# A four-layer graph network on one core: part of the first layer's row work handed to GpSimd, counts and degrees in one PSUM bank, chain steps issued in halves

## The reference

```python
x = LN(x + L0(x))   # relu([x, (adj@x + x)/deg] @ W + b), rows divided by their L2 norm; deg = rowsum(adj) + 1
x = LN(x + L1(x))   # tanh([x, t]@W1 + b1)@W2 + b2 + adj@(x@B.T) - rowsum(adj)*(x@B.T)
x = LN(x + L2(x))   # w@(x@weight) + bias; w[i,j] = adj[i,j] * 0.5**(min(deg, 100) - pos)
                    # pos: the rank of neighbour j among i's, less what is over 100
x = LN(x + L3(x))   # logmap(adj @ expmap(x)) @ kernel + bias
```

## Time and profile before

| | |
|---|---|
| median of 3 runs | 173.23 us (172.87 to 173.72) |
| profiled execution | 172.62 us, of which the span of the trace is 170.8 us |
| PE busy | 110.9 us (65%), 1230 matmuls |
| DVE busy | 105.7 us (62%), 235 instructions |
| ACT busy | 70.8 us (41%) |
| POOL busy | 46.3 us (27%) |
| HBM read | 18.00 MB |

### The profile page before, as it was taken

How to read it: one execution, slowest core, us unless ns; L and a number is a source line. 1 busy time by engine, 2 the same in 40 slices (tenths; PEclk the granted TensorE clock), 3 DMA queues, 4 the chain that set the end, 5 groups by cost and what they waited for, 6 DMA issues and landing times.

```text
span 170.8 us, 3082 instructions
## 1 busy us (share of the span) xinstructions
PE 110.9 (65%) x1230; PEld 63.5 (37%) x1244; DVE 105.7 (62%) x235; ACT 70.8 (41%) x119; POOL 46.3 (27%) x54
## 2 busy tenths in 40 slices
PE   0000279961996498669725979999989989994000
PEld 0000159730243124326402345667446734463000
DVE  0181999889999998950499101535602698718870
ACT  0030215577277556462781285254023310157550
POOL 0000002412421263020148000433500554603380
PEclk9999999997599789999985899999999999999755
DMA  4999999999999910000000000000000000000005
GB/s 97 255 250 345 307 347 263 319 331 333 332 331 339 341 40 4 0 0 4 0 4 0 0 0 4 0 4 2 0 4 0 0 2 0 0 4 0 0 0 123
DMA packets 13950, 18.73 MB, mean 110 GB/s; under 512 B 5360, under 2 KB 5488, under 8 KB 13936
## 3 DMA queue, kind: packets, MB, share of 16 engines
q1 hardware_dynamic: 7728, 9.74, 20.1%
q10 hardware_dynamic: 6208, 8.78, 17.5%
HBM read 18.00 MB, written 0.52 MB: 108 GB/s over the span
## 4 chain that ended last, share of the span: by engine, by line
PE 44%; DVE 26%; ACT 9%; DMA 7%; issue 4%; POOL 4%; SPq 2%; POOLq 1%; another core or an unknown queue 0%; DVEq 0%
PE psN L823 7%; PE psC L823 7%; DMA stage<-adj 7%; PE psS L823 6%; PE psS L880 5%; DVE AT L572 5%; DVE AT L573 4%; ACT WT L402 3%; PE psX L940 2%; POOL nroot L308 2%; PE psX L872 2%; PE psX L852 2%; PE psC L861 2%; PE psH L970 2%; PE psH L971 2%
## 5 line engine op out<-in xcount | busy, mean ns | idle before, releaser
L402 ACT ACTIVATE WT<-psC 128x1024 int16<-128x1024 f32 x32 | 31.3, 1021 | 17.2 <-PE psC L919 17.2
L289 POOL TENSOR_TENSOR root<-var,power 128x4 f32<-128x4 f32 (+1 forms) x16 | 18.9, 1183 | 46.8 <-DVE var L622 22.6
L823 PE MATMUL psS<-AT,XP 128*128 128x512 bf16 x74 | 20.4, 398 | 1.2 <-issue 1.1
L572 DVE STREAM_TRANSPOSE AT<-stage 128x1024 bf16<-128x1024 bf16 x10 | 13.1, 1311 | 11.7 <-DMA stage<-adj 11.7
L872 PE MATMUL psH<-AT,cb 128*32 128x256 bf16 x32 | 1.7, 344 | 19.3 <-DVE AT L573 19.3
L573 DVE STREAM_TRANSPOSE AT<-stage 128x1024 bf16<-128x1024 bf16 x10 | 12.7, 1275 | 0.0
L823 PE MATMUL psN<-AT,XP 128*128 128x512 bf16 x44 | 12.0, 402 | 1.0 <-DVE XP L578 0.7
L638 DVE TENSOR_TENSOR t<-psH,XB 128x256 f32<-128x256 f32 x4 | 1.7, 424 | 17.5 <-PE psH L971 10.2
L823 PEld LDWEIGHTS psS<-AT,XP 128*128 128x128 f16 x80 | 7.3, 101 | 12.4 <-issue 5.9
L302 POOL TENSOR_TENSOR XB<-X,weights 128x256 f32<-128x256 f32 x12 | 9.9, 835 | 7.0 <-DVE X L627 7.0
L914 PE MATMUL psC<-later,cb 32*32 32x512 bf16 x256 | 7.2, 398 | 6.0 <-ACT WT L402 6.0
(11 more groups left out here) (151 smaller groups left out, 229.5 us busy)
## 6 DMA issues: line engine op xcount, KB each, us to landing
stage<-adj SPq DMA_DIRECT2D x20, 256.0 KB, 15.2
stage<-adj ACTq DMA_DIRECT2D x20, 256.0 KB, 11.5
WT<-adj ACTq DMA_DIRECT2D x12, 256.0 KB, 12.7
WT<-adj SPq DMA_DIRECT2D x12, 256.0 KB, 16.9
out<-X SPq DMA_DIRECT2D x6, 64.0 KB, 1.9
weights<-weights_packed SPq DMA_DIRECT2D x1, 353.5 KB, 15.7
cb<-constants_packed SPq DMA_DIRECT2D x1, 264.2 KB, 9.8
X<-x SPq DMA_DIRECT2D x2, 128.0 KB, 7.1
```

Source lines behind the costliest of these rows:

```text
L289: nc.gpsimd.tensor_tensor(root[:, e, 0:n], var[:, e, 0:n], power[:, 0:n, 0:NR], ALU.pow).then_inc(root_ready, 1)
L402: nc.scalar.activation(WT[:, e, tiles], psC[:, PAIRS * h:PAIRS * (h + 1)], ACT.Relu).then_inc(chain_taken, 1)
L572: nc.vector.transpose(to[:, :, :, :, 0], halves[:, :, 0, :, :, 1])
L823: ins = nc.tensor.matmul(sum_bank(l, e), XP[:, l % 2, c], matrix, start=(c == 0), stop=last)
```

## The change

Four things are changed together.

1. **Finishing of chunks 0 and 1.** The squares, the centring, `combine` and the scaling of rows move from DVE to POOL (`square_relu`, `centre_relu`, `combine`, `scale_rows`); relu, the row sums and the split stay on DVE (`relu0`, `sums0`, `variance0`, `split1`), put between the transposes. Chunks 2 and 3 keep the old functions. POOL also centres x for all nodes (`XB`, 128x1024), and `weigh(e + 1)` now stands behind `scale_rows(e)` in POOL's order.
2. **One bank.** Counts, spread and degrees of all chunks use `psH`; `dense(0, e)` uses it too and waits for `deg_taken`.
3. **Chain in halves.** A step is two halves of two quarters (8+8 matmuls each), and a half waits only for its own two banks; the steps stand at other places in TensorE's and ScalarE's order.
4. **Order.** Tile 1 is loaded ahead of the constants; the second half of chunk 0's counts and sums comes before the own parts; only `b1` is centred early, the other six weights between `combine0(3)` and `normalise(0, 3)`.

```diff
 # sync
+            load_lower(1)
             sp.dma_start(cb[:].bitcast(U16), cpack).then_inc(consts_loaded, 16)
             sp.dma_start(weights[:, 0:first], wpack[:, 0:first]).then_inc(own_weights_loaded, 16)
-            for m in range(1, NR - 1):
+            for m in range(2, NR):
                 load_lower(m)
             sp.dma_start(weights[:, first:WTOT], wpack[:, first:WTOT]).then_inc(weights_loaded, 16)
 # gpsimd
+            def square_relu(e):
+                pool.wait_ge(y_ready, e + 1)
+                ye = v[:, chunk(e), 0:D]
+                nc.gpsimd.tensor_tensor(X[:, chunk(e)], ye, ye, ALU.mult).then_inc(ysq_ready, 1)
+            def centre_relu(e):
+                pool.wait_ge(ymean_ready, e + 1)
+                ye = v[:, chunk(e), 0:D]
+                step(nc.gpsimd.tensor_tensor(ye, ye, per_node(ymean[:, chunk(e)]), ALU.add))
+            def combine(e):
+                te = t[:, chunk(e)]
+                pool.wait_ge(ssroot_ready, e + 1)
+                step(nc.gpsimd.tensor_tensor(te, v[:, chunk(e), 0:D], per_node(ssroot[:, chunk(e)]), ALU.mult))
+                step(nc.gpsimd.tensor_tensor(te, te, XB[:, chunk(e)], ALU.add))
+                nc.gpsimd.tensor_tensor(X[:, chunk(e)], te, te, ALU.mult).then_inc(tsq_ready, 1)
+            def scale_rows(e):
+                pool.wait_ge(root_ready, e + 1)
+                nc.gpsimd.tensor_tensor(X[:, chunk(e)], t[:, chunk(e)], per_node(root[:, e, 0]), ALU.mult
+                                        ).then_inc(x_ready, 1)
...
+            pool.wait_ge(xmean_ready, 1)
+            nc.gpsimd.tensor_tensor(XB[:], X[:], per_node(xmean[:]), ALU.add).then_inc(xc_ready, 1)
...
 # vector
+            def relu0(e):
+                dve.wait_ge(dense_taken, e + 1)
+                nc.vector.tensor_scalar(v[:, chunk(e), 0:D], t[:, chunk(e)], 0.0, None, ALU.max).then_inc(y_ready, 1)
+            def sums0(e):
+                cs = chunk(e)
+                dve.wait_ge(y_ready, e + 1)
+                step(nc.vector.tensor_reduce(ymean[:, cs], v[:, cs, 0:D], AX_X, ALU.add))
+                nc.vector.tensor_scalar(ymean[:, cs], ymean[:, cs], -1.0 / D, None, ALU.mult).then_inc(ymean_ready, 1)
+                dve.wait_ge(ysq_ready, e + 1)
+                step(nc.vector.tensor_reduce(ss[:, cs], X[:, cs], AX_X, ALU.add))
+                nc.vector.tensor_tensor(ss[:, cs], ss[:, cs], floor[:, cs], ALU.max).then_inc(ss_ready, 1)
+            def variance0(e):
+                dve.wait_ge(tsq_ready, e + 1)
+                step(nc.vector.tensor_reduce(var[:, e, 1], X[:, chunk(e)], AX_X, ALU.add))
...
+            def split1(e):
+                dve.wait_ge(x_ready, e + 1)
+                split(1, e, X[:, chunk(e)], PART_SCALE[1])
...
 # tensor
             def counts(e, cols=slice(0, CW)):
-                if e == NE - 1:
-                    pe.wait_ge(hid_taken, 2)
-                bank = psH if e == 0 else psX
+                if e >= 1:
+                    pe.wait_ge(dense_taken, e)
...
             def chain(i):
...
-                else:
-                    pe.wait_ge(chain_taken, PAIRS * i)
...
+                for h in range(PAIRS):
+                    if i >= 1:
+                        pe.wait_ge(chain_taken, PAIRS * (i - 1) + h + 1)
+                    for q in range(PAIRS * h, PAIRS * (h + 1)):
...
             def dense(l, e):
                 if l == 0:
+                    pe.wait_ge(deg_taken, e + 1)
...
             pe.wait_ge(transposed, NB)
             counts(e, rest)
             sum_cols(e, 3, 4)
+            transpose_x(1, 1)
+            spread(e)
+            sums(1, 0, range(1, 2))
+            degrees(e)
             chain(10)
-            spread(e)
-            degrees(e)
             dense(0, e)
-            sums(1, 1, range(0, 1))
+            hidden(1)
             chain(11)
-            sums(1, 1, range(1, 2))
+            sums(1, 1, range(0, 2))
             chain(12)
             transpose_x(1, 2)
             sums(1, 0, range(2, 3))
+            chain(13)
             hidden(2)
             sums(1, 1, range(2, 3))
-            chain(13)
+            chain(14)
             sums(1, 0, late)
...
             dense(1, 0)
-            chain(14)
+            chain(15)
             sums(1, 2, every)
             add_own(1, 2)
             dense(1, 1)
-            chain(15)
```

191 lines of the change are left out of this document (99 added, 92 removed).

## The result

The kernel after takes 165.3 us (median of 4 runs, 164.39 to 165.9) against 173.06 (4 runs, 172.87 to 173.72): a ratio of 0.9541, 95% interval 0.9489 to 0.9592. The forecast was 163.9, range 160.3 to 168.5. The profiled execution took 165.22 us, its span is 163.3. Some executions of a kernel take 1.5 to 4% longer than its fastest, mostly at a lower granted clock: ratios and intervals leave them out, the times in the table of the experiments are medians of all, and the profiled executions of dense_late, whole_steps, degrees_first and late_tail are of that kind.

What follows compares the result with a forecast made beforehand. DVE was taken to bound the kernel up to tile 15's last transpose, then a chain of waits between engines. -2.2 - 6.5 - 0.6 = -9.3 us gave 163.3 profiled, 163.9 as median; range 160.3 to 168.5.

Steps and rivals of the forecast that it cites:

- E: End of tile 15's second transpose on DVE: 2.2 us earlier, at about 70.9 (bounds -6 and +3).
- TensorE can hold DVE up at `take_degrees`: DVE may wait for degrees of chunks 1 and 2: 1.2 us added, between 0 and 5.
- Rival 1: TensorE's clock falls in both groups and DVE waits 3 to 5 us for degrees: 166 to 168 us; chance 0.20.
- The other terms of E: DVE's changes up to tile 15's last transpose, without the added wait for degrees: -3.4 us together.
- Contention at the two splits: `split1` of chunks 0 and 1 meets POOL at the memory port: 1.0 us added per chunk (0 to 1.5).
- the six instructions: Row work leaving DVE per early chunk (squares, centring, three of `combine0`, row scaling): 2.7 us, 5.4 for two chunks.
- Before tile 5 nothing is gained: Start of DVE's transposes: reading is saturated, so the end of tile 5's second transpose stays at 33.49 us.
- Rival 4: POOL's port use also holds up DVE's transposes, 13 us in all: 177 us; chance 0.05 with the like.
- E to D: From tile 15's last transpose to the end of layer 1's first `dense`: 6.5 us shorter (bounds -3 and -7.5).
- Rival 3: Behind tile 15, ScalarE's six steps delay its copies and the late sums; only 3 us gained: 167.5 us; chance 0.10.
- Chain: Behind layer 1's first `dense`: one step instead of two, -0.8, plus 0.2 for halves: -0.6 us.
- The other signs: Wait near 2 us for last degrees, chunk 3's split some 18.5 us after tile 15, late sums unwaited, first `dense` 24 us after.

Runs made afterwards that it cites:

- dense_late: The kernel after, with `dense(0, 0)` moved behind the own parts and the first chain step on TensorE; 162.56 us, ratio to before 0.9400.
- whole_steps: The kernel after, with chain steps issued whole again instead of in halves; 164.80 us, ratio to before 0.9492.
- degrees_first: dense_late, with the chain steps of chunks 1 and 2 behind the degrees instead of ahead of them; 163.91 us, ratio to before 0.9436.
- late_tail: dense_late, with six weights centred during DVE's wait for the last degrees and POOL's chunk 2 root ahead of chunk 3's; 161.36 us, ratio to before 0.9292.
- counts_behind_hidden: The kernel after, with the last counts put back behind chunk 1's hidden layer and its tanh; 172.55 us, ratio to before 0.9827.
- pool_finish_2: The kernel before with only POOL's and DVE's new work and order, plus `dense(0, e)` ahead of layer 1's sums; 174.23 us, ratio to before 1.0010.

## Why the prediction was right, and where it was not

**E: -2.2 predicted, 0.0 measured. The term that failed is "TensorE can hold DVE up at `take_degrees`", mis-sized: 1.2 us taken, 4.28 measured**, inside its bounds of 0 and 5. The working had chunk 1's counts at 40.7 and its degrees at 46.0. The counts came at 44.56: the own parts took 3.62 us at the lower clock instead of some 2, `dense(0, 0)` began 0.6 later, and the second chain step waited 1.08 for ScalarE. From counts to degrees it took 6.70 instead of 5.3. The text named the low clock as the danger for counts, sum blocks and chain, priced at 2 to 3 us and taken at 1.2, but not for the own parts ahead of them. It dated the queue behind the waiting `dense(0, 0)`, but so that the degrees came just when DVE did, with nothing to spare. By the estimate from the experiments the clock accounts for 4.5 us and the queue for 0.6 to 1.6. Rival 1 had most of this, the low clock and the wait within its price of 3 to 5 us, but the clock fell in one group only (chunk 2's counts took 1.04 us at 59.61). The time fell short of its 166 to 168 since other terms of E were better than worked out.

**The other terms of E: -3.4 predicted, -5.0 measured** (a window of 38.84 us less the 4.28, against 39.57). Contention at the two splits was taken at 1.0 each. They took 1.16 and 1.15, where 0.83 was the price beside POOL before: 0.3 each. The one at 55.24 ended at 56.40, 0.3 behind the end of `diag` (54.97 + 1.15) and before that of `XB` (56.98), so DVE was held through one of POOL's instructions and not through a row of them. The Trainium skill's rule in "SBUF — State Buffer" (section "Who interferes with whom") says who is held, and the trace agrees at the splits. It does not everywhere: beside POOL's root of 128x4 (82.21, 1.01 us) DVE's centring at 82.50, which has two inputs, took its usual 0.42, and there the measurement decides. The sum went wrong in how many instructions the split was held for. The waits for degrees that went were 0.98 and 0.72, of which the text took only the first. Against that, relu, the scaling and the maximum met POOL for 0.1 to 0.5 each, and at 41.82 stands a wait of 0.58 for POOL's square: 1.4 instead of 0.6. With the six instructions at their 5.4 and the added scalings at 0.4 these terms make about -4.7; the other 0.3 stays open. POOL's added row operations are 12 and not the 10 of the working, 7.6 us in all; but for the 0.58 they cost DVE nothing beyond the port.

**"Before tile 5 nothing is gained"** was short by 0.7: tile 5 ended at 34.17 instead of 33.49, since tile 4 waited for its transfer all the same and the centring of `b1` now lies behind it. So E: 0.7 + 4.3 - 5.0 = 0.0.

**Rival 4** (transposes held by the port, 177 us) fell: the longest transpose took 1.34 us, and POOL was in time except for those 0.58.

**E to D: -6.5 predicted, -6.8 measured**, and by its steps: degrees at +4.6 (+4.5), chunk 2's parts at +12.5 (+12.7), chunk 3's at +18.4 (+18.6), late sums to D 5.23 us (5.3), D at +23.7 (+24.0). counts_behind_hidden confirms the cause of the first step. The rest has two more causes that no run tests alone: the clock was full here (1.00 against 0.89), and DVE takes chunk 2's `combine0` ahead of chunk 3's addition, an edit that the list of the change leaves out and the working uses; from the last degrees to chunk 2's parts DVE needed 7.9 us instead of 9.0. Rival 3 (ScalarE's copies push it back) fell. The late sums began 0.05 us behind the parts, as forecast, and TensorE had been idle 1.31 us for them.

**Chain: -0.6 predicted, -0.6 measured** behind D (67.2 to 66.6). The 0.2 us a step for halves was too much: 0.03. With that the sum would have been -0.8, so the agreement is in part chance.

Sum: 0.0 - 6.8 - 0.6 = -7.4 (172.62 to 165.22 in the profiled executions) against -9.3. The range held the time, and that is partly luck: two errors of opposite sign in E, 3.1 us too little waiting and 1.6 too little gained elsewhere, hid a part of the miss. By its own signs E was wrong: tile 15's second transpose ended at 73.01, not between 69.5 and 72, and DVE waited over 2 us for chunk 1's degrees. The other signs came out right. What the prediction did not see is how the parts depend on each other: it added E and E to D, and with the old order behind E a gain at E is worth nothing (pool_finish_2).

## What to carry to other kernels

When an engine's order gets a new wait, list everything that stands behind the waiting instruction and date it; here an early small product held up the own parts and the chain, and TensorE's idle time in front of it was followed by 13 us at the lower clock, which by the estimate above cost more than the queue did. A gain in one stage is kept only if the next stage's first instruction waits for that stage and not for another engine; look at who ends that wait before moving work. And compare versions by distances between events in the profile, since the start of tile 4 alone lay between 27.7 and 30.2 us; before reading a distance, look at the granted clock in it.
